# One stage in place of two between cross-attention and the routed experts of a decoder layer, with shorter routing arithmetic and a second gather buffer

## The chip, the cores and the metric

The kernel runs on one core of a Trainium2 chip. The core has five engines that run their own instruction queues in order and meet only at semaphores: TensorE (PE, matrix products), VectorE (DVE), ScalarE (ACT), GpSimd (POOL) and SyncE (SP, which mostly issues transfers). The metric is the device time of one execution in microseconds (us). All times inside an execution are counted from the start of its span.

## The reference, cut to what matters

Four sequences of 1024 tokens with 256 channels go through linear attention, softmax attention and a mixture of experts, each followed by adding the input and a layernorm. The change touches the end of the second of these and the third:

```python
x = _layernorm(x + _L0_xattn_ref(x, ctx_1024, ...))      # ends in y @ W_proj + b_proj
x = _layernorm(x + _L0_ffn_ref(x, ...))

def _route(x2d, router_weight, e_bias):                  # 16 experts in 4 groups, 2 groups, 4 experts
    scores = jax.nn.sigmoid(x2d @ router_weight.T)
    sc = scores + e_bias[None, :]
    group_scores = jnp.sum(jax.lax.top_k(sc.reshape(T, G, E // G), 2)[0], axis=-1)
    _, gidx = jax.lax.top_k(group_scores, TG)
    ...
    _, tidx = jax.lax.top_k(masked, K)
    tw = jnp.take_along_axis(scores, tidx, axis=1)
    tw = tw / (jnp.sum(tw, axis=-1, keepdims=True) + 1e-20)
    return (tidx, tw * SCALE)
# an expert and the two shared experts: silu(x @ gate) * (x @ up) @ down, inner width 128
return routed + shared
```

## The kernel before

The 4096 tokens are 32 blocks of 128 rows. Four blocks make a tile of 512 tokens (`TILE`, `TB` = 4), so there are 8 tiles (`NT`), two for each sequence. The kernel is a chain of stages, each with its own buffers and its own program for each engine; a stage begins when the stage ahead of it has ended on all engines and its transfers have landed. The names of buffers carry the stage as a prefix: `sa_` softmax attention, `cl_` the close of an attention, `ms_` shared experts and placing, `mo_` routed experts, `mp_`, `mh_`, `mr_` and `c_` buffers that outlive a stage.

Softmax attention (`softmax_attention`, `sa_`) goes through 4 sequences of 4 quads of heads. SP stores the result of each quad (L1311). In the last sequence SP also writes zeros over `xs`, the buffer of the experts' rows in device memory, in 18 transfers of 1 MB (L1300), and loads the two shared experts (L1607). The stage waits at its end for the stores and for `zeroed`.

The second close (`close_attention` with stage 2, `cl_`): for each tile POOL scales `y` by the inverse denominators (L904) and adds the bias to `x` (L905), PE projects `y` (L939), DVE adds `x` (L1081) and takes mean and variance (`layernorm_stats`, L750, L753, L755), POOL takes the inverse root (L911), DVE normalises (L1091), PE turns the tile (L986), ACT copies it (L1036), PE multiplies by the router (L967), ACT takes the sigmoid (L1041), and PE turns the scores back (L976). SP and ACT store `x3`, `xT3` and `score` to device memory.

Shared experts and placing (`share_and_place`, `ms_`): DVE works the routing out for groups of tiles (`ROUTE_TILES`). For each group `choose` finds the four experts of each token (L1842 to L1878), `weigh` their weights (L1884 to L1889) and `place_tokens` the row of each token in each expert's list (L1906 to L1932), with counts from PE (`count`, L1735 to L1739). Each expert's rows go in blocks of 128 through `xs`. POOL scatters the rows with one indirect transfer for each block and choice (L1819, 32 x 4 = 128 in all), out of a tile of `x` reloaded from `x3` into one of three buffers. Beside it PE runs the shared experts, each product in three passes of a 32-bit format with fewer bits (`three_passes`, L273 to L275), for which ACT and DVE split each operand into a high and a low part (L1794, L1938, L1802, L1945). Silu is L1798, the sums of the shared experts with `x` go to `shared` in device memory.

Routed experts (`routed_experts`, `mo_`): 72 pairs of list blocks are read from `xs` (L2034), multiplied and stored to `ys` (L2055). POOL fetches a tile's rows back with 16 indirect transfers into `picked` (L2189) as soon as the first `pairs_for(n)` pairs are stored (16, 32, 32, 48, 48, 56, 64, 72 for the 8 tiles), and takes the inverse root of the layernorm (L2179) behind the tile's fetches. DVE adds the rows up (L2211), takes the statistics and normalises (L2226), at pairs which `combine_at` fixes; the fetches of a tile wait until the tile ahead has been added up, since there is one buffer.

```python
                    if n:
                        pool.wait_ge(combined, (n - 1) * TOPK + i + 1)
```

Of the kernel before, what the change touches and what calls it, by code (L numbers as in the profile page):

```python
# [27 lines left out]
F32 = mybir.dt.float32  # L28
BF16 = mybir.dt.bfloat16
F32R = mybir.dt.float32r  # L30
I32 = mybir.dt.int32
ALU = mybir.AluOpType
# [1186 lines left out]
def softmax_attention(nc, io, given, closing, weights):  # L1219
# [5 lines left out]
    with Phase(nc, "sa") as ph:  # L1225
# [21 lines left out]
        zeroed, zero_set = ph.own("zeroed"), ph.sem("zero_set")  # L1247
# [34 lines left out]
        def _(sp):  # L1282
# [9 lines left out]
            def batch_row(b, last):  # L1292
                if last:
                    sp.wait_ge(zero_set, 1 + START)
                for g in range(QUADS):
                    if not (last and g == QUADS - 1):
                        maxima(*after(b, g))
                    if last:
                        for i in range(g * ZERO_RUNS // QUADS, (g + 1) * ZERO_RUNS // QUADS):
                            sp.dma_start(io["xs"].rearrange("(p n) c -> p (n c)", p=P)[:, i * ZERO_RUN:(i + 1) * ZERO_RUN],  # L1300
                                         zero[:, :]).then_inc(zeroed, 16)
# [15 lines left out]
            load_q(sp, 0, 1)  # L1317
            maxima(0, 0)
# [9 lines left out]
            sp.wait_ge(zeroed, 16 * ZERO_RUNS)  # L1328
# [245 lines left out]
W_SLOTS = SHARED  # L1574
ROUTE_TILES = ((0, 1), (1, 3), (3, 5), (5, 6), (6, 7), (7, 8))
# [4 lines left out]
FRESH = N_ROUTES * EXPERTS  # L1580

# [8 lines left out]
class Weights:  # L1590

    def __init__(self, nc, ph, tiles):
        self.nc = nc
        self.raw = tiles.sb("raw", [P, SHARED, EXPERT_W])
        self.w_in = ph.sems("w_in", SHARED)
        self.hi_done, self.split, self.table_in = ph.sem("hi_done"), ph.sem("split"), ph.sem("table_in")

    def add_parts(self, ph):
        self.hi = ph.sb("hi", [P, SHARED * EXPERT_W], F32R)
        self.lo = ph.sb("lo", [P, SHARED * EXPERT_W], F32R)  # L1600
        self.table = ph.sb("table", [P, EXPERTS * EXPERT_W])

    def of(self, e):
        return slice(e * EXPERT_W, (e + 1) * EXPERT_W)

    def load(self, eng, io, e):
        eng.dma_start(self.raw[:, e], io["experts"][:, e]).then_inc(self.w_in[e], 16)  # L1607

    def load_routed(self, eng, io, e):
        eng.dma_start(self.table[:, self.of(e)], io["experts"][:, SHARED + e]).then_inc(self.table_in, 16)  # L1610

    def round_up(self, act, e):
        act.wait_ge(self.w_in[e], 16)
        self.nc.scalar.activation(self.hi[:, self.of(e)], self.raw[:, e], ACT.Copy).then_inc(self.hi_done, 1)

    def remainder(self, eng, by, e):
        eng.wait_ge(self.hi_done, e + 1)
        by.tensor_tensor(self.lo[:, self.of(e)], self.raw[:, e], self.hi[:, self.of(e)].bitcast(F32), ALU.subtract).then_inc(self.split, 1)
# [12 lines left out]
def share_and_place(nc, io, weights, places):  # L1631


    w_hi, w_lo = weights.hi, weights.lo
    H_SLOTS = 3
    X_SLOTS = 3
    with Phase(nc, "ms") as ph:
        e_bias = ph.sb("e_bias", [P, MOST_BLOCKS, EXPERTS])
        score = ph.sb("score", [P, ALLB, EXPERTS])
        grank = ph.sb("grank", [P, ALLB, GROUPS])  # L1640
        ident = ph.sb("ident", [P, P])
        until_f32 = ph.sb("until_f32", [P, P])
        until, every = ph.sb("until", [P, P], BF16), ph.sb("every", [P, P], BF16)
        minus_first = ph.sb("minus_first", [FRESH, 1])
        list_rows = ph.sb("list_rows", [FRESH, NLIST])
        xT = ph.sb("xT", [P, HALVES, CT, TILE])
        x_hi, x_lo = ph.sb("x_hi", [P, HALVES, CT, TILE], F32R), ph.sb("x_lo", [P, HALVES, CT, TILE], F32R)
        x = ph.sb("x", [P, X_SLOTS, TB, C])
        silu = ph.sb("silu", [P, 2, TILE])
        h = ph.sb("h", [P, 2, TILE])  # L1650
        h_hi, h_lo = ph.sb("h_hi", [P, H_SLOTS, TILE], F32R), ph.sb("h_lo", [P, H_SLOTS, TILE], F32R)
        acc = ph.sb("acc", [P, 2, TB, C])
        biased, kept, equal, equal_kept, rank, carried, spots = (
            ph.sb(n, [P, MOST_BLOCKS, EXPERTS]) for n in ("biased", "kept", "equal", "equal_kept", "rank", "carried", "spots"))
        up_to = [ph.sb(f"up_to{i}", [P, MOST_BLOCKS, EXPERTS]) for i in range(2)]
        ones16 = ph.sb("ones16", [P, EXPERTS])
        kept_b = ph.sb("kept_b", [P, MOST_BLOCKS + 1, EXPERTS], BF16)
        largest = ph.sb("largest", [P, MOST_BLOCKS, 8])
        topmost = ph.sb("topmost", [P, MOST_BLOCKS, 8])
        match = ph.sb("match", [P, MOST_BLOCKS, TOPK, EXPERTS])  # L1660
        pair_hi, pair_lo = ph.sb("pair_hi", [P, MOST_BLOCKS, GROUPS, 2]), ph.sb("pair_lo", [P, MOST_BLOCKS, GROUPS, 2])
        g1, g2, g3, gsum, gge = (ph.sb(n, [P, MOST_BLOCKS, GROUPS]) for n in ("g1", "g2", "g3", "gsum", "gge"))
        wsum = ph.sb("wsum", [P, MOST_BLOCKS])
        counts = [ph.sb(f"counts{i}", [P, EXPERTS]) for i in range(2)]
        held = [ph.sb(f"held{i}", [P, EXPERTS]) for i in range(2)]
# [21 lines left out]
        def tile_rows(n):  # L1687
            return slice(n * TILE, (n + 1) * TILE)
# [700 lines left out]
```

## Time and profile before

| | us |
|---|---|
| median of 3 runs | 1998.46 (1998.31 to 2001.28) |
| the profiled execution | 2002.49 |
| its span (first to last instruction) | 2000.8 |
| softmax attention ends, close begins | 1359.6 |
| close | 1360 to 1451 |
| shared experts and placing | 1451 to 1669 |
| routed experts | 1669 to 2001 |

The mean TensorE clock granted over the span was 0.897 of full speed. Over the whole span PE is busy for 1593.2 us (80%), DVE 1261.6 (63%), ACT 872.8 (44%) and POOL 641.4 (32%). These shares are means over stages with different limits, so the table by stage is what to read; a stage's number of busy microseconds is to be set against its own length.

### The profile page before, as it was taken

To read this page: it belongs to the slowest core of one execution; us is meant where nothing else is said; L and a number is where in the kernel's file an instruction comes from. 1 tells how busy PE (TensorE), PEld (TensorE's weight loads), DVE (VectorE), ACT (ScalarE), POOL (GpSimd) and SP (SyncE) were. 2 spreads that over 40 slices of the span, in tenths; PEclk is the share of its full clock that TensorE was granted. 3 is DMA by queue.
4 is the path that set the end of the run, shared out by engine and by line. 5 is a ranking of instruction groups with operands and counts; after the bars stand their busy time and mean duration, and the time that the engine had idled before them with its cause. 6 is when DMAs were issued, how large, how long until landed. Compare 5 with 4: busy or idle time off the path is not lost. (4 is left out here: it accounts for less than half of the span.)

```text
span 2000.8 us, 35485 instructions
## 1 busy us (share of the span) xinstructions
PE 1593.2 (80%) x11450; PEld 933.0 (47%) x11450; DVE 1261.6 (63%) x3617; ACT 872.8 (44%) x1414; POOL 641.4 (32%) x853
## 2 busy tenths in 40 slices
PE   6968999999688789989989999975713465998860
PEld 4646676777455223323333333313413354887740
DVE  7964455555599868868878888815766650124333
ACT  5634554555133136656655666661211112554430
POOL 1134333320342511111111121125446771224654
PEclk9989999999799669989999999997957787999985
DMA  5699655672468653453353535375644564677763
GB/s 173 218 190 156 115 100 101 116 143 76 127 211 236 150 74 54 80 80 55 54 88 55 73 56 149 125 267 193 205 145 162 199 203 141 191 218 214 230 189 102
DMA packets 207503, 285.80 MB, mean 143 GB/s; under 512 B 55122, under 2 KB 162322, under 8 KB 200430
## 3 DMA queue, kind: packets, MB, share of 16 engines
q1 hardware_dynamic: 168830, 202.39, 38.0%
q0 software_dynamic: 22560, 66.62, 15.6%
q10 hardware_dynamic: 15952, 14.63, 2.8%
q8 instruction: 102, 1.67, 0.4%
q14 instruction: 59, 0.48, 0.1%
HBM read 154.24 MB, written 128.92 MB: 142 GB/s over the span
## 5 line engine op out<-in xcount | busy, mean ns | idle before, releaser
L1470 ACT ACTIVATE sa_prob<-sa_ps_s 128x1024 f32<-128x1024 f32 (+3 forms) x480 | 376.3, 825 | 284.2 <-PE sa_ps_s L1379 202.9
L1529 DVE CUSTOM_DVE_ANT_0 sa_ps_m<-sa_ps_m,sf_later 128x282 f32<-128x282 f32 (+4 forms) x640 | 278.5, 461 | 54.5 <-PE sa_ps_m L1352 53.1
L1532 DVE TENSOR_REDUCE sa_piece_max<-sa_ps_m 128x1 f32<-128x512 f32 x384 | 259.2, 688 | 45.2 <-PE sa_ps_m L1352 44.7
L1506 POOL TENSOR_SCALAR_AFFINE_SELECT sa_prob<-sa_prob 128x256 f32<-128x256 f32 x256 | 102.2, 406 | 502.9 <-ACT sa_prob L1470 500.4
L1352 PE MATMUL sa_ps_m<-sa_k,sa_q 96*128 96x512 bf16 (+4 forms) x768 | 211.8, 336 | 21.0 <-DVE sa_max_parts L1560 7.4
L1352 PEld LDWEIGHTS sa_ps_m<-sa_k,sa_q 96*128 96x128 bf16 x768 | 66.6, 99 | 242.3 <-issue 111.4
L2189 POOL DMA_INDIRECT mo_picked<-s_ys,mp_row x128 | 125.7, 982 | 134.7 <-DMA s_ys<-mo_y 95.8
L1379 PE MATMUL sa_ps_s<-sa_q,sa_k 99*128 99x512 bf16 (+3 forms) x672 | 160.8, 333 | 2.1 <-ACT sa_prob L1470 2.0
L688 ACT ACTIVATE la_phi_kT<-la_ps_kT 128x512 f32<-128x512 f32 x128 | 76.4, 597 | 190.1 <-PE la_ps_kT L624 190.1
L643 PE MATMUL la_ps_att<-la_phi_qT,la_phi_kT 128*128 128x128 f32 x1024 | 147.2, 288 | 12.7 <-issue 12.0
L735 DVE TENSOR_TENSOR la_att<-la_ps_att,lf_cap 128x512 f32<-128x512 f32 x128 | 88.3, 690 | 108.2 <-PE la_ps_att L643 108.2
L1819 POOL DMA_INDIRECT s_xs<-ms_x,mp_row x128 | 128.7, 1006 | 67.4 <-issue 38.4
L2097 PE MATMUL mo_ps_gu<-mh_table,mo_xT 128*128 x576 | 139.2, 385 | 0.0
L643 PEld LDWEIGHTS la_ps_att<-la_phi_qT,la_phi_kT 128*128 128x128 f32 x1024 | 128.3, 197 | 20.4 <-issue 17.0
L2202 DVE TENSOR_TENSOR mo_h<-mo_silu,mo_ps_gu 128x256 f32<-128x256 f32 x72 | 29.6, 419 | 149.4 <-ACT mo_silu L2145 149.4
L1396 PE MATMUL sa_ps_y<-sa_prob,sa_v 128*17 128x512 f32 (+3 forms) x1152 | 119.9, 491 | 0.3 <-POOL sa_prob L1506 0.2
L2211 DVE SCALAR_TENSOR_TENSOR mo_acc<-mo_picked,mp_weight,mo_acc 128x256 f32<-128x256 f32 x128 | 53.6, 480 | 92.9 <-DMA mo_picked<-s_ys,mp_row 92.9
L2097 PEld LDWEIGHTS mo_ps_gu<-mh_table,mo_xT 128*128 128x128 f32 x576 | 106.3, 195 | 12.3 <-issue 0.3
L939 PE MATMUL cl_ps_o<-c_w,cl_yn 128*128 128x256 f32 x256 | 73.0, 450 | 34.7 <-POOL cl_yn L904 34.7
L1352 PE MATMUL sa_ps_m<-sf_k,sf_q 96*128 96x512 bf16 (+4 forms) x256 | 78.6, 364 | 17.1 <-SPq L115 8.4
L1529 DVE DVE_READ_ACCUMULATOR2_ANT sa_piece_max<- 128x1 f32 x640 | 90.8, 149 | 0.0
L152 POOL DMA_DIRECT2D la_q<-s_q_parts x72 | 35.4, 504 | 168.4 <-DVE la_y L740 130.0
(289 smaller groups left out, 3130.9 us busy)
## 6 DMA issues: line engine op xcount, KB each, us to landing
s_xs<-sa_zero SPq DMA_DIRECT2D x18, 1024.0 KB, 9.9
mo_rows<-s_xs SPq DMA_DIRECT2D x72, 256.0 KB, 4.2
s_ys<-mo_y SPq DMA_DIRECT2D x72, 256.0 KB, 2.7
la_q<-s_q_parts POOLq DMA_DIRECT2D x72, 128.0 KB, 5.9
la_k<-s_k_parts POOLq DMA_DIRECT2D x72, 128.0 KB, 7.7
sa_q<-s_q_parts SPq DMA_DIRECT2D x72, 128.0 KB, 5.0
sa_k<-s_k_parts SPq DMA_DIRECT2D x66, 128.0 KB, 7.2
s_y<-la_y SPq DMA_DIRECT2D x16, 512.0 KB, 3.5
```

Of the source, the lines that this page charges most:

```text
L643: last = nc.tensor.matmul(ps_att[:, j], phi_kT[:, d, j], phi_qT[:, d, j], start=True, stop=True)
L735: nc.vector.tensor_tensor(att[:, c % 2], ps_att[:, :, :], cap[:, :, :], ALU.min).then_inc(att_done, 1)
L1352: nc.tensor.matmul(ps_m[:, s, 0:hi - lo], qs, k[g][0:STACK, j, PAD + lo:PAD + hi], start=True, stop=True, skip_group_check=True).then_inc( ...
L1379: last = nc.tensor.matmul(ps_s[:, s, jj, 0:TILE - first], keys, q[g][:, j, queries], start=True, stop=True)
L1396: last = nc.tensor.matmul(ps_y[32 * j:32 * j + V1, first:TILE], values, prob[:, prob_slot(g, units[j // 2]), j % 2, 0:TILE - first], start ...
L1470: nc.scalar.activation(dst, src, ACT.Exp, scale=HD ** -0.5).then_inc(expd[s], 1)
L1506: nc.gpsimd.affine_select(out=square, in_=square, compare_op=ALU.is_ge, fill=0.0, base=0, pattern=[[0, 2], [1, P]], channel_multiplier=-1) ...
L1529: nc.vector.tensor_tensor_reduce(ps_m[:, s, 0:hi - lo], ps_m[:, s, 0:hi - lo], later[:, BANK + lo - first:BANK + hi - first], 1.0, -BIG, A ...
L1532: nc.vector.tensor_reduce(piece_max[:, j, t, n:n + 1], ps_m[:, s, 0:hi - lo], AX.X, ALU.max).then_inc(piece_done[s], 1)
L1819: nc.gpsimd.indirect_dma_start(io["xs"], bass.IndirectOffsetOnAxis(ap=rows, axis=0), x[:, n % X_SLOTS, t], None).then_inc(scattered[n], 16)
L2097: last = nc.tensor.matmul(ps_gu[:, q % 2, s * C:(s + 1) * C], xT[:, q % 2, a, s * P:(s + 1) * P], table[:, at], start=a == 0, stop=a == CT ...
L2189: nc.gpsimd.indirect_dma_start(picked[:, i, t], None, io["ys"][0:pairs_for(n) * COLS], bass.IndirectOffsetOnAxis(ap=at, axis=0)).then_inc( ...
```

## The change

The second close and the placing become one stage, `close_and_place`, written out tile by tile. `share_and_place`, the class `Weights`, and the stores and loads of `x3`, `xT3` and `score` go; the normalised rows of all 8 tiles stay in `xn` and are scattered from there. DVE takes over the scaling and the bias (`prepare`), ACT the normalising, and POOL keeps the inverse roots (`root`) and the scatters. The scores come straight from matrix products with 16 columns (`rate`). The shared experts are one plain f32 product each. `choose` compares the sums of all six pairs of a group's members, and finds the experts with `max_index`; `place_tokens` works from the one-hot `match`. The groups of tiles change. The zeros are written over all 16 quads, one transfer of 1.18 MB each, and only POOL waits for them, ahead of its first scatter. All 18 experts are loaded in the new stage. In the routed experts `picked` has two sets, `pairs_for` gives 16, 24, 40, 40, 56, 56, 64, 72, and the roots move in between the fetches of the next tile. `combine_at` gives first pairs of 20, 28, 44, 51, 60, 67, 74 and 81, and the normalising comes four pairs behind the sums and not three.

```diff
-ROUTE_TILES = ((0, 1), (1, 3), (3, 5), (5, 6), (6, 7), (7, 8))
+ROUTE_TILES = ((0, 1), (1, 2), (2, 4), (4, 6), (6, 7), (7, 8))
# softmax_attention, SP
-                    if last:
-                        for i in range(g * ZERO_RUNS // QUADS, (g + 1) * ZERO_RUNS // QUADS):
-                            sp.dma_start(io["xs"]...[:, i * ZERO_RUN:(i + 1) * ZERO_RUN], zero[:, :]).then_inc(zeroed, 16)
-                        for e in range(g * W_SLOTS // QUADS, (g + 1) * W_SLOTS // QUADS):
-                            weights.load(sp, io, e)
+                    sp.dma_start(io["xs"]...[:, bass.ds(quad_before(b, g) * ZERO_RUN, ZERO_RUN)], zero[:, :]).then_inc(zeroed, 16)
...
-            sp.wait_ge(zeroed, 16 * ZERO_RUNS)
# close_and_place, PE
+            out_project(0)
+            for n in range(NT + 2):
+                if n < NT:
+                    turn(n)
+                    rate(n)
+                if n >= 2:
+                    project_down(n - 2, 0)
+                if n + 1 < NT:
+                    out_project(n + 1)
+                if n >= 2:
+                    project_down(n - 2, 1)
+                if 1 <= n <= NT:
+                    gate_up(n - 1, 0)
+                if n < NT and group_at(n) is not None:
+                    count(group_at(n))
+                if 1 <= n <= NT:
+                    gate_up(n - 1, 1)
# ACT
+            normalise(0)
+            for n in range(NT + 1):
+                if n < NT:
+                    act.wait_ge(t_ps, n + 1)
...
+                    nc.scalar.activation(xT[:, n % 2], ps_t[:, :, :], ACT.Copy).then_inc(t_done, 1)
+                    act.wait_ge(s_ps, n + 1)
+                    nc.scalar.activation(score[:, n * TB:(n + 1) * TB], ps_score[:, n % 2], ACT.Sigmoid).then_inc(scored, 1)
+                if n:
+                    activate((n - 1) * SHARED)
+                    activate((n - 1) * SHARED + 1)
+                if n + 1 < NT:
+                    normalise(n + 1)
# POOL
+            root(0)
+            done = 0
+            for n in range(NT):
+                if n + 1 < NT:
+                    root(n + 1)
+                scatter(done, scattered_by(n))
+                done = scattered_by(n)
# DVE
+            for n in range(NT + 2):
+                g = group_at(n)
+                if g is not None:
+                    choose(g)
+                if n >= 2:
+                    add_up(n - 2, 0)
+                if n + 1 < NT:
+                    sum_up(n + 1)
+                if n >= 2:
+                    add_up(n - 2, 1)
+                if 1 <= n <= NT:
+                    multiply((n - 1) * SHARED)
+                if g is not None:
+                    place_tokens(g)
+                    weigh(g)
+                if 1 <= n <= NT:
+                    multiply((n - 1) * SHARED + 1)
+                if n + 1 < NT:
+                    centre(n + 1)
+                if n + 2 < NT:
+                    prepare(n + 2)
# routed_experts, POOL
-            for n in range(NT):
-                for s in range(SLOTS):
-                    pool.wait_ge(y_out[s], -(-(pairs_for(n) - s) // SLOTS) * 16)
-                for i in range(TOPK):
-                    if n:
-                        pool.wait_ge(combined, (n - 1) * TOPK + i + 1)
...
-                root(n)
+            def fetch(n, i):
+                if i == 0:
+                    for s in range(SLOTS):
+                        pool.wait_ge(y_out[s], -(-(pairs_for(n) - s) // SLOTS) * 16)
+                if n >= 2:
+                    pool.wait_ge(combined, (n - 2) * TOPK + i + 1)
...
+            for n in range(NT):
+                late = n and pairs_for(n) <= combine_at(n - 1, TOPK - 1)
+                if n and not late:
+                    root(n - 1)
+                fetch(n, 0)
+                fetch(n, 1)
+                if late:
+                    root(n - 1)
+                fetch(n, 2)
+                fetch(n, 3)
+            root(NT - 1)
```

`group_at(n)` is the group that ends with tile n: groups end at the tiles 0, 1, 3, 5, 6 and 7, and those that end at 3 and 5 hold two tiles. `scattered_by(n)` is how many scatters POOL has issued behind `root(n + 1)`: 13, 29, 32, 61, 64, 93, 109 and 128 for the 8 tiles.

## Rows read from the trace of the kernel before

**Rows 1.** Busy time by stretch: start:end, length, each engine's, granted clock, DMA share, GB/s
```profile
1340.00:1360.00 20.00, 0.00 (x0) 0.00 (x0) 0.20 (x1) 0.83 (x2) 0.00 (x0) 0.54 0.74 294
1360.00:1451.00 91.00, 64.67 (x256) 43.87 (x256) 61.53 (x122) 16.41 (x27) 49.18 (x27) 0.86 0.63 200
1451.00:1659.00 208.00, 82.02 (x426) 67.37 (x426) 127.57 (x529) 28.61 (x41) 132.73 (x133) 0.70 0.53 175
1669.00:1814.00 145.00, 141.43 (x776) 123.60 (x777) 33.15 (x86) 74.99 (x171) 32.18 (x34) 0.98 0.67 206
```
**Rows 2.** Timeline of SP's queue at the end of attention: start, time to issue, transfer
```profile
1333.97 5.16 SPq L1300 DMA_DIRECT2D s_xs<-sa_zero  x5
1340.70 1.17 SPq L1311 DMA_DIRECT2D s_y<-sa_y  x1
```
**Rows 3.** Transfers issued in 1340 to 1365: count, size, median us to landing
```profile
s_y<-sa_y SPq DMA_DIRECT2D x1, 512.0 KB, 17.8
```
**Rows 4.** The page's transfers: count, size, median us to landing
```profile
s_ys<-mo_y SPq DMA_DIRECT2D x72, 256.0 KB, 2.7
...
s_y<-la_y SPq DMA_DIRECT2D x16, 512.0 KB, 3.5
```
**Rows 5.** Groups of instructions in 1360 to 1669, by shape: busy, mean ns, idle before
```profile
L1819 POOL DMA_INDIRECT s_xs<-ms_x,mp_row x128 | 128.7, 1006 | 67.4 <-issue 38.4 <-DVE mp_row L1924 28.7 <-DMA ms_x<-s_x 0.3
...
L1938 DVE TENSOR_TENSOR ms_x_lo<-ms_xT,ms_x_hi 128x1024 fp32r<-128x1024 f32 x8 | 9.7, 1224 | 22.9 <-ACT ms_x_hi L1794 22.9
```
**Rows 6.** Timeline of DVE, one tile of the close, then parts of the routing
```profile
1400.41 1.29 DVE L1081 TENSOR_TENSOR cl_z<-cl_ps_o,cl_xb 128x512 f32<-128x512 f32 x2
...
1405.10 6.82 DVE L1091 TENSOR_SCALAR cl_xn<-cl_z,cl_moments,cl_rstd 128x256 f32<-128x256 f32 x4 [1.34 <-POOL cl_rstd L911]
...
1467.55 0.22 DVE L1907 TENSOR_TENSOR ms_rank<-ms_ps_rank,ms_counts 128x64 f32<-128x64 f32 x1
...
1471.24 0.18 DVE L1924 TENSOR_SCALAR mp_row<-ms_topmost 128x16 int32<-128x16 f32 x1
...
1472.42 0.43 DVE L1931 TENSOR_TENSOR ms_match<-ms_match,ms_equal 128x256 f32<-128x256 f32 x1
```
**Rows 7.** Timeline of PE in the close at the higher clock
```profile
1411.97 1.10 PE L986 MATMUL cl_ps_t<-c_ident,cl_xn 128*128 128x128 f32 x8 [1.70 <-DVE cl_xn L1091]
...
1413.34 3.62 PE L939 MATMUL cl_ps_o<-c_w,cl_yn 128*128 128x256 f32 x16
1416.88 1.91 PE L967 MATMUL cl_ps_r<-cl_xT,c_router 128*32 128x512 f32 x4
```
**Rows 8.** Busy time by stretch in the placing, columns as above
```profile
1500.00:1512.00 12.00, 0.00 (x0) 0.00 (x0) 10.12 (x49) 1.57 (x2) 9.19 (x9) 0.59 0.28 99
1512.00:1515.00 3.00, 2.79 (x14) 2.36 (x15) 2.62 (x13) 0.00 (x0) 1.92 (x2) 0.50 0.30 108
```
**Rows 9.** Timeline of POOL: a long scatter, and the first work behind the last one
```profile
1492.36 2.02 POOL L1819 DMA_INDIRECT s_xs<-ms_x,mp_row  x1 [0.30 <-issue]
...
1669.13 0.10 POOL L2174 MEMSET mo_power<- 128x4 f32 x1 [10.92 <-POOLq L83]
```
**Rows 10.** Timeline of ACT in the placing
```profile
1468.47 1.28 ACT L1798 ACT_TABLE_LOAD   x1
1495.43 0.60 ACT L1798 ACTIVATE ms_silu<-ms_ps_g 128x512 f32<-128x512 f32 x1 [25.68 <-PE ms_ps_g L275]
```
**Rows 11.** Timeline of SP's queue, the first stores of the routed experts
```profile
1683.57 0.36 SPq L2055 DMA_DIRECT2D s_ys<-mo_y  x1
...
1686.82 0.36 SPq L2055 DMA_DIRECT2D s_ys<-mo_y  x1
```
**Rows 12.** Timeline of POOL: a tile's fetches, the root behind them, the last fetch
```profile
1817.98 1.00 POOL L2189 DMA_INDIRECT mo_picked<-s_ys,mp_row  x1 [0.19 <-issue]
...
1845.03 1.04 POOL L2179 TENSOR_TENSOR mo_rstd<-mo_var,mo_power 128x4 f32<-128x4 f32 x1 [6.88 <-DVE mo_var L755]
...
1985.83 1.14 POOL L2189 DMA_INDIRECT mo_picked<-s_ys,mp_row  x1 [0.30 <-issue]
```

More of the change, by code:

```diff
@@ L1587, in pairs_for, with group_at, scattered_by @@
     return min(PAIRS, -(-(last * TB * TOPK + EXPERTS - 1) // 2))
[L1590 to L1618, printed above, removed]
+def group_at(tile):
+    return {hi - 1: g for g, (lo, hi) in enumerate(ROUTE_TILES)}.get(tile)
+def scattered_by(n):
+    ready = max((hi for lo, hi in ROUTE_TILES if hi <= n + 1), default=0) * SCATTERS
+    return min(ready, (n + 1) * SCATTERS - 3) if n < NT - 1 else NT * SCATTERS
 class Places:
@@ L1836, in _, with prepare, sum_up, centre @@
             link = chain.link
+            def prepare(n):
+                half = n % HALVES
+                dve.wait_ge(landed[half], (n // HALVES + 1) * 16 * LOADS + START)
+                tt(y[:, half], y[:, half], inv[:, half], ALU.mult).then_inc(scaled, 1)
+                tt(x[:, half], x[:, half], bias[:, :, :], ALU.add).then_inc(biased_x, 1)
+            def sum_up(n):
+                dve.wait_ge(o_ps, n + 1)
+                dve.wait_ge(biased_x, n + 1)
+                for t in range(0, TB, 2):
+                    last = tt(xn[:, n, t:t + 2], ps_o[:, t:t + 2], x[:, n % HALVES, t:t + 2], ALU.add)
+                last.then_inc(summed, 1)
+                dve.wait_ge(summed, n + 1)
+                if n >= 2:
+                    dve.wait_ge(normed, n - 1)
+                layernorm_stats(nc, dve, chain, xn[:, n], stats[:, n % 2], moments[:, n % 2], var[:, n % 2]).then_inc(var_ready, 1)
+            def centre(n):
+                dve.wait_ge(rooted, n + 1)
+                nc.vector.scalar_tensor_tensor(shift[:, n % 2], moments[:, n % 2, :, 0], -1.0, rstd[:, n % 2], ALU.mult, ALU.mult).then_inc(shifted, 1)
             def choose(g):
@@ L1857, in choose @@
-                link(ts(gge[:, 0:n], place, float(TOP_GROUPS), None, ALU.is_lt))
-                per = EXPERTS // GROUPS
-                for i in range(per):
-                    last = tt(biased[:, 0:n, i::per], biased[:, 0:n, i::per], gge[:, 0:n], ALU.mult)
-                link(last)
+                members = biased[:, 0:n].rearrange("p n (g m) -> p n g m", g=GROUPS)
+                pairs = couples[:, 0:n]
+                tt(pairs[:, :, :, 0:3], members[:, :, :, 0:3], members[:, :, :, 1:4], ALU.add)
@@ L1862, in choose @@
+                link(ts(biased[:, 0:n], biased[:, 0:n], 0.0, None, ALU.add))
                 for i in range(n):
@@ L2278, in decoder_layer @@
         linear, softmax = LinearFirst(whole), SoftmaxFirst(whole)
+        zeroed = whole.own("zeroed")
         linear_tiles = Phase(nc, "lf")
```

490 lines of the change are left out of this document (234 added, 256 removed).

## Prediction

> **What bounds the kernel now.** I read the table of busy time by stretch first, since a share over the whole span mixes stages with different limits. It shows four stretches that matter. From 1340 to 1360 no engine works, and only the DMA does [rows 1]. The close takes 91 us, in which PE is busy for 65, DVE for 62 and POOL for 49. The placing takes 208 us, in which POOL is busy for 133, DVE for 128 and PE for 82. None of them fills its stage, so these stages are bound by waits between engines, and work of the one could lie beside work of the other. The first part of the routed experts is bound by PE, 141 of 145 us.
>
> Then SP's timeline and the list of transfers for the empty stretch. The last 512 KB of attention are issued at 1340.7, behind five 1 MB transfers of zeros [rows 2], and take 17.8 us to land [rows 3]; elsewhere the same size lands in 3.5 [rows 4]. Then POOL's timeline: behind the last scatter it has nothing for 10.9 us until the routed experts begin at 1669.13 [rows 9]. In the late part of the routed experts a tile's 16 fetches take from 1817.98 to 1838.15, and then POOL waits 6.88 us for the variance [rows 12]: the fetches of the next tile stand behind a root that needs this tile's sums.
>
> **The end of attention.** The zeros move to all 16 quads, 1.18 MB each, and attention no longer waits for them. The last store then lands 17.8 - 3.5 = 14.3 us earlier; I take 14. The zeros cost DMA time in the earlier quads, 16 x 1.18 MB, as much as the 18 transfers before; PE and ACT set the pace there, and if it were not hidden the gain would go. Bounds: 0 and 15. The new stage begins at 1359.6 - 14 = 1345.6.
>
> **The new stage, prices at the higher clock.** `sum_up`: 1.29 for the sums, and with the statistics from 1400.41 to 1403.76 (the wait for the root begins there) 3.35; the root comes 1.34 later [rows 6]. `prepare`: two operations of 128x1024, 1.22 each [rows 5], beside the chain of the next tile. An operation on 16 elements for each partition is .18, on 64 .22, on 256 .43 [rows 6], and I add .04 between two that depend on each other. `choose` for four blocks has twelve of 16 to 96 elements (12 x .26 = 3.1), eight short ones of `max` and `max_index`, which don't wait for each other (half a step each: .9) and two of 256 (.94): 4.9. `place_tokens` has seven of 16, five of 64, two of 256 and the cast: 4.1 until the rows are known, .6 behind that. `weigh`: 2.0. For eight blocks I take 7.0, 5.0 and 2.5. `turn` is 1.1, `out_project` 3.6, four records of 128x512 are 1.91 [rows 7]: such a product is two records, so `gate_up` has 4 x .85 = 3.4 an expert; `project_down` is 1.7 a half, as `out_project`. `rate` is not in the trace: eight products of 16 columns. It is no shorter than eight turns, 1.1, whose blocks are wider; at `out_project`'s .226 a record, 16 of them are 3.6. I take 1.6, nearer to the turns, which have the same weight loads.
>
> **Tile by tile.** From `centre` of a tile to its scores: normalise 1.4, turn 1.1, copy 1.0, rate 1.6, sigmoid .3, five handovers: 6.5. The first `centre` comes at 14.6 (scaling, a first projection at half speed 7, sums 3.35, root). From there DVE's queue sets the order. A tile with a group of four has 6.5 + choose 4.9 + two halves of `add_up` 1.3 + sum_up 3.35 + multiply .7 + place 4.7 + weigh 2.0 + multiply .7 + .2 = 24.3, and some .7 for PE's lateness: 25. With eight blocks 28.5. Without a group PE sets it: 6.3 + 1.7 + 3.6 + 1.7 + 3.4 + .6 + 3.4 + .6 + .9 = 22. The first two have fewer parts, 21.7 and 23.7.
>
> POOL: 128 scatters in 128.7 us, 1.006 each, and .30 between them [rows 5, 9]: I take 1.29. Its roots stand in one queue with them, and this is the wait that the change adds: `root(5)` is behind 29 scatters, `root(7)` too, 37.4 us each, and `centre` of these tiles waits for it. The rows of the group that ends at tile 3 are known at 14.6 + 21.7 + 23.7 + 22 + 23.8 = 105.8 (23.8 is the part of a tile up to there). 29 scatters and root(5) bring `centre(5)` to 144.5, 12 us after DVE could have done it; 23.8 later the next group is known, 29 scatters and root(7) end at 206.8, and 35 scatters behind it at 252. POOL has little idle time from tile 3 on, so DVE and PE beside it are covered.
>
> TensorE's clock: in 1500 to 1512 PE did nothing, and in the next 3 us the granted clock was .50, the lower level of 1.2 GHz [rows 8]; the two stages had .86 and .70 over all [rows 1]. In the new stage PE waits in each tile. Some 14 us of a tile on the path are PE's at the higher clock; at a mean of .78, between .70 and .86, they take 4 more. Five tiles count (0 to 3, and 5; the others lie under the scatters): 20, less 4 that tile 4's wait for the root covers. So 252 + 16 = 268. At the lower level all the way 12 a tile: 312. Full clock: 252. With rate at 3.6 it is 10 more, at 1.1 2 less.
>
> ACT goes from Sigmoid to Silu and back in each tile, and loads a table each time. The load before took 1.28 us right behind the instruction ahead of it, and Silu waited for PE until 1495 anyway [rows 10]; here the one lies beside `rate` and the other beside 5 us of projections. I take nothing; uncovered it would be 1.28 on five tiles, 6.
>
> The Trainium skill, "ScalarE: Activation LUTs", section "What ACT_TABLE_LOAD costs", adds a drain of about 1.38 us to the 1.28, so 2.66 a switch; that speaks against alternating. By it a load would outlast `rate` by about 1 us, and the estimate for five tiles is 5 us more; the rows show no drain.
>
> The routed experts then begin at 1345.6 + 268 + 10.9 = 1624.5 in place of 1669.1: 44.6 earlier.
>
> **The routed experts.** The first store is issued at 1683.57, one each 3.25 [rows 11], and lands in 2.7 [rows 4]. On the old time scale pair 55 has landed at 1683.6 + .4 + 2.7 + 55 x 3.25 = 1865.4. That is what tile 4 waits for. With two sets and the roots between the fetches, POOL then has 64 fetches of 20.17 / 16 = 1.26 [rows 12] and four roots: 1865.4 + 80.7 + 4.9 = 1951. Pair 71 has landed at 1917, so the fetches set the end. Before, the last began at 1985.83 and ended at 1987, and 13.8 us of sums, root and store followed to the end of the span at 2000.8; these stay: 1964.8, so 36 us. Sums that come late would stop PE's queue through DVE's; but pair 55 is ahead of that. Bounds: 0, if a root still waits for sums at each tile, and 40.
>
> **Sum.** 44.6 + 36 = 80.6 off the profiled execution's 2002.5 gives 1922; its time lies 4 above the median, so against 1998.5 I forecast 1918.
>
> **The rivals.**
> A, the clock stays up through the stage: 252 and not 268, 1902. PE's work per tile is 17 of 25 us; against it is the low clock after each wait.
> B, the second set brings nothing in the routed experts: 1954. For it: DVE adds up in a fixed order, and a late sum holds PE and so the stores. Against it: the 6.88 us wait goes by construction.
> C, PE at the lower level all through the new stage: 312, 1962.
> D, DVE's large operations hold up POOL's scatters. One scatter took 2.02 in place of .96 [rows 9]. From tile 3 on 93 scatters are on the path, and if every second one is such, it costs 46 x 1.06 = 49: 1967. Against it: DVE was busy for 128 of 208 us in the placing, and the mean is still 1.006 [rows 1, 5].
> E, slower: the in-order queues lock step by step, so that in a tile no engine works beside another. A tile's work is PE 17 at the higher clock and some 27 at the mixed and lower one, DVE 18, ACT 4 and POOL 1, so 40 to 50. With seven tiles at p the stage is 14.6 + 7p + 45; all gains are eaten at 268 + 81 = 349, so at p = 41.3. At 48 it is 396, +128 on the forecast: 2046. Against it: `out_project` of the next tile and `gate_up` of the one before stand between a tile's own steps.
> That the change doesn't do what it says would show as stores of `x3` or a wait for zeros; the code leaves no room for it.
>
> By the Trainium skill, "SBUF — State Buffer", section "SBUF: two separate sides", DVE operations that take both ports lock GpSimd out while it writes the descriptors of its transfers. That is D's mechanism; the mean of 1.006 above speaks against its deciding here.
>
> **How the numbers follow.** Forecast .58 (1890 to 1945), A .12, B .10, C .08, D .06, E .06. The range takes in the forecast, A, B and C: 1890 to 1962. Under 1890 would need both bounds at once. A difference under .2% can't be told from none. Faster .93, same .01, slower .06.
>
> **What would show it.** The first projection begins near 1347; the last scatter ends 268 after the stage begins; scatters keep 1.29; `centre(5)` and `centre(7)` wait for POOL by about 10 us each; the fetches of tiles 4 to 7 run on at 1.26 with only roots between. It would be wrong if a tile in the new stage took over 30 us, if scatters grew over 1.4, or if PE's pace in the routed experts fell below one pair in 3.25 ahead of pair 55.

## The result and the profile after

The changed kernel takes 1923.51 us (median of 4 runs, 1920.70 to 1927.21), the kernel before 1998.38 in the same count of runs. The ratio is 0.9625, with a 95% interval of 0.9604 to 0.9645, so 75 us less. The forecast was 1918 with a range of 1890 to 1962. The profiled execution took 1920.70, with a span of 1919.0.

The table sets the profiled executions side by side. A stage's start is the first work that any engine does in it.

| stretch | before | after | change | forecast |
|---|---|---|---|---|
| span's start to the last copy of attention's result | 1340.5 | 1336.6 | -3.9 | 0 |
| from there to the new stage (the close, before) | 19.2 | 3.7 | -15.4 | -14 |
| the stage or the two stages, to the start of the routed experts | 309.5 | 280.9 | -28.6 | -30.6 |
| of that, behind the last scatter | 10.9 | 4.5 | -6.4 | 0 |
| routed experts to the end of the span | 331.7 | 297.8 | -33.9 | -36 |

The first line is no effect of the change: attention's own stretch, from its first copied result to its last, is 599.2 before and 599.5 after, and the difference lies ahead of it, in stages that no kernel here touches. The same last copy ends at 1335.4 to 1343.7 in the kernels below. Without this line the profiles give 78 us, near the 75 of the medians.

No run takes back the merging of the two stages, the shorter routing or the plain f32 products by itself, so how the 28.6 us of the stage divide among them is not shown.

Busy time by stretch, after: start:end, length, busy time of PE, PE's weight loads, DVE, ACT and POOL with the number of instructions, granted clock, DMA share, GB/s. It answers [rows 1].

```profile
1336.60:1340.40 3.80, 0.00 (x0) 0.00 (x0) 0.00 (x0) 0.03 (x1) 0.03 (x1) 1.00 0.34 138
1340.40:1616.80 276.40, 182.64 (x616) 129.15 (x616) 138.84 (x503) 54.11 (x78) 135.94 (x137) 0.73 0.43 135
1616.80:1621.20 4.40, 0.41 (x2) 0.09 (x2) 0.99 (x4) 0.00 (x0) 0.00 (x0) 0.92 0.43 151
1621.20:1760.00 138.80, 135.62 (x737) 118.37 (x738) 36.59 (x99) 70.87 (x162) 33.91 (x35) 0.97 0.67 207
1760.00:1906.00 146.00, 103.99 (x560) 89.74 (x559) 66.45 (x188) 55.62 (x127) 99.68 (x101) 0.86 0.75 232
```

The 20 us in which only the DMA worked are 3.8. The new stage still has no engine that fills it: PE is busy for 183 of 276 us at a mean clock of .73, DVE for 139 and POOL for 136. So the bound is again a chain through several engines.

POOL's timeline in the new stage, after: start, duration, instruction, and the idle time ahead of it with what ended it. Most scatters are left out; they stand .30 apart, but for the two idle times in the last group.

```profile
1351.97 1.04 POOL L1825 TENSOR_TENSOR ms_rstd<-ms_var,ms_power 128x4 f32<-128x4 f32 x1 [11.49 <-DVE ms_var L756]
...
1376.81 1.13 POOL L1836 DMA_INDIRECT s_xs<-ms_xn,mh_row  x1 [3.79 <-DVE mh_row L1955]
...
1460.15 1.02 POOL L1836 DMA_INDIRECT s_xs<-ms_xn,mh_row  x1 [7.14 <-DVE mh_row L1955]
...
1497.51 1.04 POOL L1825 TENSOR_TENSOR ms_rstd<-ms_var,ms_power 128x4 f32<-128x4 f32 x1
...
1519.37 1.04 POOL L1825 TENSOR_TENSOR ms_rstd<-ms_var,ms_power 128x4 f32<-128x4 f32 x1 [16.05 <-DVE ms_var L756]
1527.56 1.02 POOL L1836 DMA_INDIRECT s_xs<-ms_xn,mh_row  x1 [7.14 <-DVE mh_row L1955]
...
1565.24 1.04 POOL L1825 TENSOR_TENSOR ms_rstd<-ms_var,ms_power 128x4 f32<-128x4 f32 x1
...
1593.88 0.96 POOL L1836 DMA_INDIRECT s_xs<-ms_xn,mh_row  x1 [3.59 <-DVE mh_row L1955]
1598.10 0.96 POOL L1836 DMA_INDIRECT s_xs<-ms_xn,mh_row  x1 [3.27 <-issue]
...
1621.22 0.10 POOL L2206 MEMSET mo_power<- 128x4 f32 x1 [4.46 <-POOLq L84]
```

The two roots with no idle time ahead of them, at 1497.51 and 1565.24, are root(5) and root(7). They stand directly behind 29 scatters. Between them POOL idles for 16.05 and 7.14 us: it is first too late for DVE and then waits for DVE. Near the end it waits 3.59 us for the rows of tile 7, and 3.27 more behind that group's first scatter, for which the profile names no releaser. DVE's side of it, the centring of tiles 5 and 7, after:

```profile
1498.58 0.16 DVE L1872 SCALAR_TENSOR_TENSOR ms_shift<-ms_moments,ms_rstd 128x4 f32<-128x4 f32 x1 [8.97 <-POOL ms_rstd L1825]
...
1566.32 0.16 DVE L1872 SCALAR_TENSOR_TENSOR ms_shift<-ms_moments,ms_rstd 128x4 f32<-128x4 f32 x1 [4.73 <-POOL ms_rstd L1825]
```

PE's timeline for `turn` and `rate` of tile 4, after:

```profile
1466.06 1.97 PE L1710 MATMUL ms_ps_t<-c_ident,ms_xn 128*128 128x128 f32 x8 [8.04 <-ACT ms_xn L1793]
1469.14 3.59 PE L1719 MATMUL ms_ps_s<-c_router,ms_xT 128*128 128x16 f32 x16 [1.11 <-ACT ms_xT L1809]
```

A turn of the close took 1.10 at the higher clock [rows 7]. In all eight tiles turn takes 1.97 and the scores 3.59 or 3.60, and both come right behind a wait.

POOL's timeline in the routed experts, after: the first fetch of tile 4, a root between fetches, and the last root. It answers [rows 12].

```profile
1820.19 0.94 POOL L2221 DMA_INDIRECT mo_picked<-s_ys,mh_row  x1 [10.88 <-DMA s_ys<-mo_y]
...
1851.54 1.03 POOL L2211 TENSOR_TENSOR mo_rstd<-mo_var,mo_power 128x4 f32<-128x4 f32 x1
...
1911.63 1.03 POOL L2211 TENSOR_TENSOR mo_rstd<-mo_var,mo_power 128x4 f32<-128x4 f32 x1 [5.66 <-DVE mo_var L756]
```

The last fetch ends at 1911.63 - 5.66 = 1905.97. From 1820.19 to there are the 64 fetches of tiles 4 to 7 and the roots between them, 85.8 us. No root in between has idle time ahead of it.

### The profile page after: what moved, and what is told of

It reads as the page before. It is cut to its first block and busy times, and to the rows that moved or that the text cites. A ratio compares the mean times of both kernels' runs of the same rounds, so it can differ in the third digit from the quotient of the medians.

```text
span 1919.0 us, 34993 instructions
## 1 busy us (share of the span) xinstructions
PE 1618.9 (84%) x11386; PEld 945.7 (49%) x11386; DVE 1211.6 (63%) x3472; ACT 880.5 (46%) x1424; POOL 597.0 (31%) x830
## 5 line engine op out<-in xcount | busy, mean ns | idle before, releaser
L2221 POOL DMA_INDIRECT mo_picked<-s_ys,mh_row x128 | 126.0, 984 | 143.9 <-DMA s_ys<-mo_y 107.1
L1836 POOL DMA_INDIRECT s_xs<-ms_xn,mh_row x128 | 127.6, 997 | 62.0 <-issue 40.0
L1373 PEld LDWEIGHTS sa_ps_s<-sa_q,sa_k 99*128 99x128 bf16 x672 | 56.3, 98 | 44.3 <-ACT sa_prob L1464 16.8
L691 ACT ACTIVATE la_phi_qT<-la_ps_qT 128x512 f32<-128x512 f32 x128 | 75.7, 592 | 0.0
```

What stands on the lines that cost most here:

```text
L1373: last = nc.tensor.matmul(ps_s[:, s, jj, 0:TILE - first], keys, q[g][:, j, queries], start=True, stop=True)
L1836: nc.gpsimd.indirect_dma_start(io["xs"], bass.IndirectOffsetOnAxis(ap=rows, axis=0), xn[:, n, t], None).then_inc(scattered, 16)
L2221: nc.gpsimd.indirect_dma_start(picked[:, n % 2, i, t], None, io["ys"][0:pairs_for(n) * COLS], bass.IndirectOffsetOnAxis(ap=at, axis=0)).th ...
```

## The experiments

Each changes the kernel after the change, unless it says otherwise. "Stage" is the new stage from its start to the start of the routed experts, read from each run's trace. It is 280.9 in the changed kernel, and 280.9 to 284.5 in the five kernels that leave it as it is, so less than 4 us there mean nothing. To the end of the last scatter it is 276.4 to 277.5 in these five, which is the steadier measure.

### Which of the two edits in the routed experts counts

One gather set, with the roots where the change puts them (the two places that index the set follow):

```diff
-        picked = ph.sb("picked", [P, 2, TOPK, TB, C])
+        picked = ph.sb("picked", [P, 1, TOPK, TB, C])
...
-                if n >= 2:
-                    pool.wait_ge(combined, (n - 2) * TOPK + i + 1)
+                if n >= 1:
+                    pool.wait_ge(combined, (n - 1) * TOPK + i + 1)
...
```

> One gather set in the changed kernel, the fetches of tile n wait for the sums of tile n - 1, choice by choice; the roots stay between the fetches. Theory (the gain of 34 us in the routed experts came from moving the root, since the sums of choice i are done long before POOL has fetched the other three choices): routed experts 298 us, at most 3 more, so 1923 to 1927. Rival (the second set carried the gain): the fetches of each of the last four tiles wait for sums, and the stage goes back to some 332, so about 1957.

Measured: 1924.72, ratio to the kernel before 0.9627 (0.9611 to 0.9643); routed experts 297.6 against 297.8.

Two sets, with the root behind its own tile's fetches:

```diff
-                if n and not late:
-                    root(n - 1)
                 fetch(n, 0)
                 fetch(n, 1)
-                if late:
-                    root(n - 1)
                 fetch(n, 2)
                 fetch(n, 3)
-            root(NT - 1)
+                root(n)
```

> Two gather sets as in the changed kernel, but the root of tile n stands behind the four fetches of tile n, as before. Theory (the root holds the queue): tiles 4, 5 and 6 each lose the 6 to 7 us that POOL waits for the variance, so 18 to 21 us more, 1942 to 1945. Rival (the sets carried the gain): no more than 3 us, 1923 to 1927.

Measured: 1960.69, 0.9817 (0.9793 to 0.9840); routed experts 332.3. That is the 331.7 of the kernel before. POOL's timeline of this run, the roots of tiles 3 to 6 (columns as above):

```profile
1831.98 1.03 POOL L2211 TENSOR_TENSOR mo_rstd<-mo_var,mo_power 128x4 f32<-128x4 f32 x1 [6.99 <-DVE mo_var L756]
...
1863.51 1.04 POOL L2211 TENSOR_TENSOR mo_rstd<-mo_var,mo_power 128x4 f32<-128x4 f32 x1 [10.06 <-DVE mo_var L756]
...
1894.83 1.03 POOL L2211 TENSOR_TENSOR mo_rstd<-mo_var,mo_power 128x4 f32<-128x4 f32 x1 [9.57 <-DVE mo_var L756]
...
1922.22 1.04 POOL L2211 TENSOR_TENSOR mo_rstd<-mo_var,mo_power 128x4 f32<-128x4 f32 x1 [5.93 <-DVE mo_var L756]
```

And of the run with one set, the roots of tiles 3 to 5:

```profile
1830.66 1.24 POOL L2211 TENSOR_TENSOR mo_rstd<-mo_var,mo_power 128x4 f32<-128x4 f32 x1
...
1852.53 1.03 POOL L2211 TENSOR_TENSOR mo_rstd<-mo_var,mo_power 128x4 f32<-128x4 f32 x1
...
1874.68 1.17 POOL L2211 TENSOR_TENSOR mo_rstd<-mo_var,mo_power 128x4 f32<-128x4 f32 x1
```

In the changed kernel all of the gain in the routed experts goes with the moved root, and none with the second set: with one set no fetch of the last four tiles waits for sums, and no root between them. The new `pairs_for` and `combine_at` are in both runs. With the root behind its own fetches they bring nothing (332.3 against 331.7); whether the moved root would bring as much without them was not tried. My estimate of 18 to 21 for the root was too low. I had counted three tiles at 6 to 7 us; four tiles wait, and the later pairs at which the sums are due make it 6 to 10 (6.99 + 10.06 + 9.57 + 5.93 = 32.6, of the 34.5 between the two kernels).

### The zeros

```diff
-                    sp.dma_start(io["xs"]...[:, bass.ds(quad_before(b, g) * ZERO_RUN, ZERO_RUN)], zero[:, :]).then_inc(zeroed, 16)
+                    if last:
+                        for i in range(4 * g, 4 * g + 4):
+                            sp.dma_start(io["xs"]...[:, i * ZERO_RUN:(i + 1) * ZERO_RUN], zero[:, :]).then_inc(zeroed, 16)
```

> The zeros of the changed kernel all in the last sequence, four transfers of 1.18 MB in each of its quads, with no wait at the end of attention. Theory (the last store stands behind the zeros in the transfer engines): the last 512 KB land some 14 us later than in the changed kernel and the new stage begins as much later, so about 1937. Rival (only the wait for the zeros cost time): no change, 1923.

Measured: 1939.20, 0.9699 (0.9680 to 0.9718), so 16 us more than the changed kernel. SP's timeline of this run, and of its transfers the last store (count, size, us to landing):

```profile
1332.93 3.89 SPq L1299 DMA_DIRECT2D s_xs<-sa_zero  x4
1338.32 0.34 SPq L1307 DMA_DIRECT2D s_y<-sa_y  x1
1355.64 0.58 SPq L1667 DMA_DIRECT2D ms_den<-s_y  x1
```
```profile
s_y<-sa_y SPq DMA_DIRECT2D x1, 512.0 KB, 16.2
```

No one waits for the zeros at the end of attention in this kernel, and still the next stage begins 17.4 us behind the last copy (1338.3 to 1355.6), as against 3.7. So what costs time is the place of the last store behind 4.7 MB of zeros: it costs 13.6 of the 15.4 us again without any wait for the zeros.

### The roots behind the scatters

```diff
-    return min(ready, (n + 1) * SCATTERS - 3) if n < NT - 1 else NT * SCATTERS
+    return (13, 29, 32, 48, 64, 80, 109, 128)[n]
```

> The scatters of the two groups of eight blocks are split, 16 of them behind the root of the next tile and not ahead of it (POOL has issued 13, 29, 32, 48, 64, 80, 109 and 128 by the 8 tiles). Theory (the root stands behind 29 scatters, DVE waits 9.0 us for it in tile 5 and 4.7 in tile 7, and POOL idles later): both waits go, and the stage ends 10 to 14 us earlier, 1909 to 1913. Rival (from tile 3 on the number of scatters sets the end): no change, 1923.

Measured: 1913.14, 0.9572 (0.9536 to 0.9609); stage 270.1, so 10.8 less. DVE's timeline of this run, the centring of tiles 5 and 7:

```profile
1492.42 0.16 DVE L1871 SCALAR_TENSOR_TENSOR ms_shift<-ms_moments,ms_rstd 128x4 f32<-128x4 f32 x1
...
1554.15 0.16 DVE L1871 SCALAR_TENSOR_TENSOR ms_shift<-ms_moments,ms_rstd 128x4 f32<-128x4 f32 x1
```

Both waits for a root are gone. The number of scatters is the same, so it is not their number alone that sets the end, but that the roots are queued behind them.

### The tables of ACT

```diff
-                nc.scalar.activation(silu[:, k % 2], ps_g[:, :], ACT.Silu).then_inc(silu_done, 1)
+                nc.scalar.activation(silu[:, k % 2], ps_g[:, :], ACT.Sigmoid).then_inc(silu_done, 1)
```

> The shared experts of the new stage use Sigmoid in place of Silu, so that ACT loads no table in it (the output of the shared experts is another function). Theory (the 14 loads lie beside work of PE): no change, 1922 to 1925. Rival 1 (a drain of 1.38 us besides, by the Trainium skill): 5 us less, 1918. Rival 2 (each load on the path): 12 to 18 us less, 1906 to 1911.

Measured: 1923.71, 0.9626 (0.9587 to 0.9664); stage 281.1. Of the 14 loads 13 go (the first one, to Sigmoid, stays, and one moves to the start of the routed experts), and the time is the same, so they cost nothing here. ACT's timeline in tile 1, after:

```profile
1387.61 0.23 ACT L1811 ACTIVATE ms_score<-ms_ps_s 128x64 f32<-128x64 f32 x1 [3.68 <-PE ms_ps_s L1719]
1387.85 1.28 ACT L1801 ACT_TABLE_LOAD   x1
1395.02 0.60 ACT L1801 ACTIVATE ms_silu<-ms_ps_g 128x512 f32<-128x512 f32 x1 [5.88 <-PE ms_ps_g L1747]
```

The load begins .01 behind the sigmoid, and ACT then waits 5.88 us for PE. The drain of which the Trainium skill speaks ("ScalarE: Activation LUTs", section "What ACT_TABLE_LOAD costs") would lie inside such a wait. No drain is to be seen ahead of the load, and by this run it has no price in this kernel.

### The clock of PE

Products of no use go ahead of each tile's turn, into the bank that turn will overwrite:

```diff
             def turn(n):
-                pe.wait_ge(normed, n + 1)
                 if n:
                     pe.wait_ge(t_done, n)
+                for _ in range(WARM[n]):
+                    nc.tensor.matmul(ps_t[:, 0, 0:P], ident[:, :], ident[:, :], start=True, stop=True, skip_group_check=True)
+                pe.wait_ge(normed, n + 1)
```

First with (40, 80, 45, 18, 50, 80, 50, 80) of them for the eight tiles.

> PE gets products of no use (128 columns, 18 to 80 of them) ahead of each tile's turn in the new stage, while it would wait for the normalised rows. Theory (PE is at the lower clock of 1.2 GHz after each wait, and turn and scores lie on the path): turn 1.97 goes to 1.1 and the scores 3.6 to 1.8, so 2.7 us for each of the five tiles that count, and some more for the projections: the new stage 12 to 20 us shorter, 1903 to 1911. Rival (the scores are bound by loading the weights, at either clock): 3.6 stays, and at most 5 us are won, 1918 or above. If the added products outlast the wait, the time goes up by what they take.

Measured: 1927.72, 0.9648 (0.9626 to 0.9670); stage 287.2. At the higher clock turn takes 1.04 in all tiles and the scores 1.96 in six of them, so the scores are not bound by something that the clock leaves alone. But an added product is two records and cost .226, not the .137 that I had taken from eight turns. Tile 1 of this run, ACT's normalising and then PE's additions and turn:

```profile
1377.22 2.07 ACT L1796 ACTIVATE ms_xn<-ms_xn,ms_shift,ms_rstd 128x256 f32<-128x256 f32 x4 [15.47 <-DVE ms_shift L1875]
```
```profile
1367.40 18.11 PE L1709 MATMUL ms_ps_t<-c_ident 128*128 128x128 f32 x160
1385.34 1.04 PE L1713 MATMUL ms_ps_t<-c_ident,ms_xn 128*128 128x128 f32 x8
```

The additions outlasted the normalising in all eight tiles, by .9 to 6.0 us and most in 1, 7 and 5. The test was spoilt by its dose. Then with (26, 46, 26, 9, 30, 46, 30, 44):

> As the first run with added products, but fewer of them (9 to 46), so that they end before the rows are normalised. There turn took 1.04 and the scores 1.96 at the higher clock, and yet the stage was no shorter, since in the tiles 1, 5 and 7 turn began 3 to 5 us later than without. Theory (the clock costs 2.7 us in each tile on the path): with shorter additions tile 5's rows are known 10 to 14 us earlier and the new stage ends 10 to 16 us earlier, 1907 to 1913. Rival (what DVE and POOL do beside sets the stage's length, and a faster PE only waits longer): 1919 or above.

Measured: 1916.75, 0.9579 (0.9544 to 0.9614), between theory and rival; stage 273.8. In six tiles the scores still took 3.46 to 3.60, behind the waits that were left: 1.0 to 4.8 us ahead of turn and 1.11 between turn and scores. A third version fills both, with (20, 42, 20, 4, 24, 46, 24, 44) of the same products in the first place (`keep_busy` issues them):

```diff
...
+                keep_busy(ps_t[:, 0, 0:P], WARM[n])
+                pe.wait_ge(shifted, n + 1)
+                keep_busy(ps_t[:, 0, 0:P], 9)
                 pe.wait_ge(normed, n + 1)
...
                 last.then_inc(t_ps, 1)
+                if n >= 3:
+                    pe.wait_ge(added, (n - 2) * 2)
+                keep_busy(ps_d[:, 0, 0:P], 4)
```

> The changed kernel with products of no use in all of PE's waits ahead of the scores: until the centring of the tile, through the normalising (9), and between turn and scores (4), so that the higher clock holds over both. In the second run with added products the scores had still taken 3.6 in six of eight tiles, and the stage was 7 us shorter. Theory (turn and scores at the lower clock cost 2.6 us in each of the five tiles on the path): turn 1.0 and scores 2.0 in all tiles, the stage 13 us shorter than in the changed kernel, 1908 to 1913. Rival (only the first tiles matter, behind tile 3 POOL's scatters set the end): 7 to 9 us, 1914 to 1918, as before.

Measured: 1914.02, 0.9572 (0.9536 to 0.9607); stage 270.4, so 10.5 less, between theory (13) and rival (7 to 9); the time is at the rival's edge (1914 to 1918). PE's timeline of this run, tile 4 and then tile 5 (the additions beside the normalising, and the second half of `project_down`), and then POOL's, the rows of the group that ends at tile 3, root(5), and the rows of the next group:

```profile
1457.54 1.09 PE L1718 MATMUL ms_ps_t<-c_ident,ms_xn 128*128 128x128 f32 x8
1459.75 1.96 PE L1730 MATMUL ms_ps_s<-c_router,ms_xT 128*128 128x16 f32 x16 [0.22 <-ACT ms_xT L1820]
...
1490.27 3.60 PE L1707 MATMUL ms_ps_t<-c_ident 128*128 128x128 f32 x18 [4.42 <-DVE ms_shift L1883]
...
1506.72 2.47 PE L1768 MATMUL ms_ps_d<-mh_table,ms_h 128*128 128x256 f32 x8 [3.32 <-DVE ms_acc L1984]
```
```profile
1451.64 1.02 POOL L1847 DMA_INDIRECT s_xs<-ms_xn,mh_row  x1 [8.85 <-DVE mh_row L1966]
...
1488.97 1.04 POOL L1836 TENSOR_TENSOR ms_rstd<-ms_var,ms_power 128x4 f32<-128x4 f32 x1
...
1519.79 1.02 POOL L1847 DMA_INDIRECT s_xs<-ms_xn,mh_row  x1 [8.84 <-DVE mh_row L1966]
```

The stage begins at 1344.1 in this run. The rows of the group that ends at tile 3 are scattered from 107.5 on; in the changed kernel it was 119.8 (1460.15 - 1340.37). So 12.3 us are won in four tiles, 3.1 each. Behind that nothing more is won, as the rival had it: root(5) to the next group's rows is 29.8 against 29.0, and the last scatter ends 12.3 us earlier too. Tile 5 is no clean test of the clock, since the additions ended too soon there: behind a wait of 4.42 us their last 18 records took 3.60 in place of 2.27 and held up the turn, and a second wait of 3.32 us stands ahead of `project_down`.

### Groups of one tile

```diff
-ROUTE_TILES = ((0, 1), (1, 2), (2, 4), (4, 6), (6, 7), (7, 8))
+ROUTE_TILES = ((0, 1), (1, 2), (2, 3), (3, 4), (4, 5), (5, 6), (6, 7), (7, 8))
```

> Eight groups of one tile each in place of six, so the rows of a tile are scattered as soon as they are known, and the routed experts fetch a tile's rows from pair 16, 24, 32, ... 72. Theory: the scatters come at 16 a tile (21 us of some 29), no root waits behind 29 of them, DVE has 16 us more of routing but waits for no root: new stage 5 to 17 us shorter; in the routed experts tile 7 starts at pair 71 and not behind three other tiles, 10 to 14 us: 1892 to 1908. Rival (the small operations of DVE are the bound, and more groups add to them): stage 10 us longer, 1920 or above.

Measured: 1896.24, 0.9476 (0.9442 to 0.9510). The stage is 270.1, the routed experts 282.6, so 10.8 and 15.2 less (`pairs_for` follows from the groups, so both stages change). And with the third version's additions (20, 42, and 20 in each tile behind):

> Groups of one tile each (1896) together with the added products in all of PE's waits ahead of the scores. There no root stands behind more than 16 scatters, and each tile has the same loop of about 30 us: centre, normalise, turn, scores, choice, sums, places. Theory (the loop is one chain, so what PE saves at the higher clock is saved in each tile): 2.6 us for turn and scores and up to 1.3 for the projection behind them, eight times, 20 to 30 us: 1866 to 1876. Rival (DVE's own work of about 23 us a tile and POOL's set the loop): at most 8 us, 1888 or above.

Measured: 1873.60, 0.9360 (0.9327 to 0.9393), the fastest of all. Busy time by stretch of the new stage (columns as above), first of the groups of one and then of those with the additions:

```profile
1346.30:1616.40 270.10, 184.65 (x620) 130.86 (x620) 153.99 (x590) 54.08 (x78) 134.52 (x138) 0.73 0.45 141
```
```profile
1347.40:1594.20 246.80, 214.57 (x1192) 165.87 (x1192) 154.24 (x590) 54.10 (x78) 134.88 (x137) 0.95 0.49 154
```

In the groups of one DVE does 15 us more than in the changed kernel (154 against 139), and still the stage is shorter; no root stands behind more than 16 scatters now, which fits the run with sooner roots. With the additions the clock is at .95 in place of .73, DVE and POOL do the same work, and the stage is 23.3 us shorter, as the theory of one chain had it (20 to 30). PE's share shows how little its busy time says: it is 30 us busier.

## Why the prediction held, and where its steps were off

The forecast was right in direction and within 6 us in size, with the waits that it named, but part of its closeness is luck: errors of 8.4 and 6.4 us inside the new stage have opposite signs. By its steps:

**The end of attention.** 14 forecast, 15.4 measured, by the mechanism that was named; the run with the zeros in the last sequence takes 13.6 of it back. Spread over 16 quads the zeros take nothing that shows: attention's own stretch, from its first copied result to its last, is 599.2 before and 599.5 after.

**The tile.** From `centre` to the scores it had 6.5 at the higher clock; it is 9.3 (1431.18 to 1440.48 in tile 3): normalise 2.08 and not 1.4, turn 1.97 and not 1.1, scores 3.60 and not 1.6. The rows of the group that ends at tile 3 were to be known at 105.8 at the higher clock, plus 16 for the clock in four tiles; the changed kernel has 119.8, so 14.0 more, and the third run with additions, at 107.5, wins 12.3 of them back. So the size of the clock term held in these tiles. What was wrong is the picture of a mean clock of .78 over 14 us of PE's work: the granted clock is no mean that all work shares. In this kernel turn and scores come behind waits of 3.0 to 12.2 us and 1.11 us and always run at 1.2 GHz, and they are what the others wait for; the projections behind them run mostly at 2.4 GHz (in tile 5 the granted clock is .50 from 1498.5 to 1508, .80 from there to 1516 and 1.00 to 1528), and in tile 5 all but 1.8 us of them lie beside work of DVE.

The Trainium skill, "TensorE: Matmul & The Clock Gate", section "HAM oscillation — how this bites in real kernels", describes a matmul kernel whose PE is back at the lower clock for each burst of products, because it waits for transfers in between. The trace agrees in kind, though the waits here are for other engines: the scores take 3.59 in the changed kernel, and 1.96 in the third run with additions, which fills the waits.

**The groups of eight.** From root(5) to the next group's rows the forecast had 23.8 at the higher clock, and the changed kernel has 29.0. DVE's timeline, after, in tile 5, the start of `choose` and the first `multiply`, and PE's, the second half of `project_down`:

```profile
1507.88 0.29 DVE L1879 TENSOR_TENSOR ms_biased<-ms_score,ms_e_bias 128x128 f32<-128x128 f32 x1 [6.87 <-ACT ms_score L1811]
...
1521.67 0.69 DVE L1966 TENSOR_TENSOR ms_h<-ms_silu,ms_ps_u 128x512 f32<-128x512 f32 x1 [1.79 <-issue]
```
```profile
1516.18 1.97 PE L1757 MATMUL ms_ps_d<-mh_table,ms_h 128*128 128x256 f32 x8 [1.45 <-DVE ms_acc L1973]
```

Of the 5.2 us too many, 2.8 lie between root and scores, as in every tile. Another 1.8 are the wait ahead of `multiply`: the second half of `project_down` waits for the first half's sum, which stands behind `choose` of eight blocks in DVE's queue; `gate_up` and `multiply` stand behind that, and the rows behind `multiply`. The forecast added .7 for such lateness in a group of four and nothing in one of eight. The rest is mostly .5 in `choose` and .3 in `place_tokens`.

**The scatters and their roots.** The pitch was 1.29, as forecast (127.6 us for 128, .997 each). The wait that the change adds was named and is there: 9.0 and 4.7 us, where about 10 were forecast for each; sooner roots win 10.8. The forecast of 268 for the last scatter became 276.4, the largest miss in the sum, and it lies in two terms. The forecast took 20 us for the clock in five tiles, which cost 14.0 + 5.2 = 19.2, but gave 4 back because tile 4's wait for the root covers them. Tile 4 was not among the five, and nothing came back: from the rows of one group to the end of root(5) POOL takes 38.4, as forecast (38.7). And the 35 scatters behind root(7) were to take 45.2 and take 50.5, since POOL waits there for the rows of tile 7 (3.59) and behind their first scatter (3.27); the forecast had no wait in this place. In the third run with additions it is 49.7, with waits of 2.74 and 3.27; what the 3.27 are is open.

One of the forecast's own signs of being wrong came out: from one `centre` to the next the tiles 3 to 6 take 32.6, 34.8, 32.6 and 35.2 us, where over 30 was to speak against it. Its own sum has 28.5 + 4 = 32.5 for the tiles 3 and 5, and more for 4 and 6, from the waits for a root; so the sign was set too low.

**The gap.** 10.9 was carried over from before, and 4.5 is what it takes now: DVE's last operation ends at 1618.4, and the routed experts begin 2.9 behind it; in the other runs it is 2.3 to 3.0, while the last scatter ends 4.1 to 7.2 ahead of them. So the start is not set by the scatters. The list of first blocks (`mh_first`) and the last store of the shared experts' sums end the stage together, and no run tells which of them counts:

```profile
1616.55 0.38 SPq L1688 DMA_DIRECT2D s_shared<-ms_acc  x1
...
1618.06 0.30 DVE L2021 CAST mh_first<-ms_ps_g 1x144 int32<-1x144 f32 x1 [0.50 <-PE ms_ps_g L1786]
```

Why it was 10.9 before is open; the trace shows no engine and no transfer at work in the last 9 us of it. This error of 6.4 hid, by luck, most of the 8.4 us by which the last scatter came later.

**The routed experts.** 36 forecast, 33.9 measured. 64 fetches and their roots were to take 85.6 and took 85.8, with 13.0 behind them and not 13.8. The fetches of tile 4 began 199.0 into the stage and not 196.3: the first store came at 15.5 and not 14.4, and the last of the 56 landed later. The mechanism was half right: the text gave the gain to the two sets and the roots together, and rival B priced a second set that brings nothing at 36 us. The set brings nothing, and the 33.9 us came all the same, with the root.

**The rivals.** A, the clock up through the stage, did not happen and, made to happen (.94 over the stage in the third run with additions), gives 1914 and not 1902. C was near for turn and scores, and wrong for the rest. D did not happen: DVE is busy for half of the stage, and a scatter takes .997 in the mean; the rule of the Trainium skill ("SBUF — State Buffer", section "SBUF: two separate sides") on locked ports shows at most in single ones: three took 1.83 to 2.03, each beside `prepare`'s operations of 128x1024 on DVE. E did not happen: the engines' busy times add up to 512 us in 276.

## What to carry to other kernels

An engine's queue is in order, so a short instruction on which others wait must not be queued behind long work that no one waits for: a root of 1 us behind 29 scatters cost 11 us here, and one behind each tile's fetches 35, while a second buffer brought nothing. Large transfers that are not urgent cost time by standing ahead of a small urgent one, even if no one waits for them. In a chain through several engines, price PE's work right behind its waits at the lower clock unless a trace shows otherwise, and test a tile's loop by keeping PE busy with products of no use; their count has to be taken from a measured price.

## What was not expected of the hardware

Products in f32 with 16 columns cost about as much as those with 128: `rate`'s 16 records take 3.59 at the lower clock, .225 each, and 1.96 at the higher, .122; a record of the added products with 128 columns took .113 there. With 256 columns, 16 records take 6.66 and 3.62 [rows 7]. In the second run with additions two tiles with nearly the same waits came out differently: 1.28 us ahead of turn and 1.11 ahead of the scores in tile 2, whose scores took 1.96, and 1.02 and 1.11 in tile 3, whose scores took 3.60. And a turn behind a wait of 3.03 took 1.97 in tile 3 of the changed kernel, while one behind 3.02 took 1.09 in tile 5 of the run with sooner roots.
